# Conv, residual and a mixed 64x64 product per sample: each load queue takes one block of channels over the whole length, with fillers of TensorE moved and the last unit cut by half pairs

## The reference

```python
out0 = conv1d(x, weight, pad 4, 9 taps, 4 groups of 16 channels)    # weight: 64 x 16 x 9
x    = x + out0 + (cond @ c_weight.T)[:, :, None] + bias[None, :, None]
h    = gelu(cond @ W0 + b0); h = gelu(h @ W1 + b1)
att  = softmax(h @ W2 + b2)                                         # 8 experts, per sample
mix  = einsum('bk,koi->boi', att, W)                                # a 64x64 matrix per sample
x    = x + einsum('boi,bih->boh', mix, x) + (att @ bias_k)[:, :, None]
```

## Time and profile before

| | us |
|---|---|
| median of 3 executions | 248.54 (248.18 to 249.06) |
| the profiled execution, whole | 249.11 |
| the profiled execution, span | 247.3 |
| TensorE busy within the span | 237.3 (96%) |
| VectorE busy | 220.3 (89%) |
| ScalarE busy | 126.6 (51%) |
| GpSimd busy | 10.4 (4%) |

### The profile page before, as it was taken

How to read it: one execution, slowest core, us unless ns; L and a number is a source line. 1 busy time by engine, 2 the same in 40 slices (tenths; PEclk the granted TensorE clock), 3 DMA queues, 4 the chain that set the end, 5 groups by cost and what they waited for, 6 DMA issues and landing times.

```text
span 247.3 us, 5763 instructions
## 1 busy us (share of the span) xinstructions
PE 237.3 (96%) x2162; PEld 103.9 (42%) x2162; DVE 220.3 (89%) x113; ACT 126.6 (51%) x208; POOL 10.4 (4%) x36
## 2 busy tenths in 40 slices
PE   6799999999999999999999999999999999999991
PEld 4643334344344444444444444444444444444530
DVE  1075899999999999999999999999999999999582
ACT  2457007374535456383645445373745446263772
POOL 1325000000000000000000000000000000000000
PEclk9689999999999999999999999999999999999999
DMA  7998566999999999999999999999999997444448
GB/s 189 307 326 240 152 125 191 258 312 365 357 322 268 359 263 383 249 380 238 334 294 292 327 256 378 247 388 239 362 273 322 298 281 293 170 170 172 171 184 328
DMA packets 28555, 68.39 MB, mean 277 GB/s; under 512 B 3184, under 2 KB 3568, under 8 KB 28544
## 3 DMA queue, kind: packets, MB, share of 16 engines
q1 hardware_dynamic: 19104, 50.98, 62.3%
q10 hardware_dynamic: 9440, 17.26, 26.5%
HBM read 34.67 MB, written 33.55 MB: 276 GB/s over the span
## 4 chain that ended last, share of the span: by engine, by line
PE 91%; DVE 3%; ACTq 2%; ACT 1%; issue 1%; DVEq 0%
PE yps L528 64%; PE zps L551 21%; PE yps L608 3%; DVE ynat L433 2%; ACTq L285 2%; PE yps L565 1%; PE zps L577 1%; DVE ycol L424 1%; PE yps L509 0%; PE yps L623 0%; PE yps L588 0%; ACT mixt L317 0%; DVE xin L498 0%; PE zps L588 0%; ACT L324 0%
## 5 line engine op out<-in xcount | busy, mean ns | idle before, releaser
L528 PE MATMUL yps<-xph,wraw 64*64 64x512 f32 x1512 | 169.0, 589 | 0.0
L303 ACT ACTIVATE zout<-zps,gamu 128x512 f32<-128x512 f32 x120 | 72.7, 688 | 95.3 <-PE zps L551 75.6
L528 PEld LDWEIGHTS yps<-xph,wraw 64*64 64x64 f32 x1512 | 67.5, 132 | 94.0 <-issue 94.0
L424 DVE STREAM_TRANSPOSE ycol<-yps 128x1024 f32<-128x1024 f32 x63 | 75.2, 1224 | 7.0 <-PE yps L528 5.4
L402 DVE STREAM_TRANSPOSE xph<-xin 128x4160 f32<-128x4160 f32 (+2 forms) x17 | 71.7, 4220 | 5.1 <-DMA xin<-in_x 5.1
L433 DVE STREAM_TRANSPOSE ynat<-ycol 128x4096 f32<-128x4096 f32 x15 | 66.7, 4446 | 1.1
L551 PE MATMUL zps<-ynat,mixv 64*64 64x512 f32 x480 | 57.8, 589 | 0.3 <-DVE ynat L433 0.3
L312 ACT ACTIVATE mixv<-mixt 64x256 f32 (+1 forms) x64 | 42.4, 663 | 1.4 <-ACT mixt L317 0.2
L551 PEld LDWEIGHTS zps<-ynat,mixv 64*64 64x64 f32 x480 | 21.6, 133 | 29.9 <-issue 29.6
L608 PE MATMUL yps<-zout 128*128 128x256 f32 x26 | 10.4, 566 | 1.3 <-POOL zout L243 1.3
L241 POOL COPY gamu<-gam 128x4 f32 (+1 forms) x16 | 2.9, 188 | 199.9 <-ACT zout L303 191.8
(11 more groups left out here) (56 smaller groups left out, 34.8 us busy)
## 6 DMA issues: line engine op xcount, KB each, us to landing
out<-zout SPq DMA_DIRECT2D x60, 512.0 KB, 6.2
xin<-in_x SPq DMA_DIRECT2D x64, 258.0 KB, 7.2
xin<-in_x ACTq DMA_DIRECT2D x64, 258.0 KB, 7.4
out<-xin SPq DMA_DIRECT2D x2, 512.0 KB, 2.7
out<-xin SPq DMA_DIRECT2D x4, 256.0 KB, 3.0
mlps<-in_mlp SPq DMA_DIRECT2D x1, 233.5 KB, 2.8
wraw<-in_conv_w ACTq DMA_DIRECT2D x1, 208.0 KB, 3.7
zout<-in_const_w SPq DMA_DIRECT2D x1, 160.0 KB, 9.3
```

The lines of the kernel that those rows point to most:

```text
L303: nc.scalar.activation(zout[:, o].rearrange("p (i c j q) -> p c i j q", i=2, c=2, q=PH)[:, c], zps[:, at:at + BANK].rearrange("p (q i j) - ...
L424: nc.vector.transpose(ycol[:, :, :, :, :, g].rearrange("p i s j q c -> p (i s j) q c"), yps[:, 2 * BANK * (g % 2):2 * BANK * (g % 2) + 2 * ...
L528: last = nc.tensor.matmul(yps[C * c:C * c + C, at:at + BANK].rearrange("p (s f) -> p s f", s=S // 2), wsum[rows, b, g], xph[slot][rows, g, ...
```

## The change

- **Loads.** SP brings block k = 0 of the channels and ACT block k = 1, each for both halves of the length. Order within a queue: samples t = 0 with half 0 and half 1, then t = 1 with half 0 and half 1. The DMAs are the same 128 pieces.
- **ScalarE's start.** The dummy Gelu stands right behind `conv_w`'s issue, ahead of `mix_w` and x of unit 0. ACT's part of unit 1 is issued as two DMAs behind `h1` and two behind `beta`.
- **Fillers.** One more behind the first two products of the chain, one more behind the product for `h2`; of the three behind `output_constants`, two move ahead of it and one stays.
- **The last unit.** All four pairs are mixed, emptied and stored by half pairs, in the order of `LAST`. ScalarE empties the first six, VectorE the last two; SP issues eight stores of 256 KB in place of two of 512 KB and four of 256 KB.

```diff
+LAST = (0, 0), (2, 0), (0, 1), (2, 1), (1, 0), (3, 0), (1, 1), (3, 1)
 def z_half(o, i):
-    return (yps, zps)[i][:, BANK * (o - 1):BANK * (o - 1) + 2 * BANK].rearrange(
-        "p (c h f) -> p h c f", c=2, h=2)[:, 0]
+    bank, at = {(0, 0): (zps, 0), (2, 0): (yps, 2), (0, 1): (zps, 2), (2, 1): (zps, 0),
+                (1, 0): (yps, 0), (3, 0): (yps, 2), (1, 1): (zps, 2), (3, 1): (zps, 0)}[o, i]
+    return bank[:, BANK * at:BANK * at + 2 * BANK].rearrange("p (c h f) -> p h c f", c=2, h=2)[:, 0]
 # SyncE: load
-                for k in range(KQ):
-                    for t in range(2):
-                        sp.dma_start(*x_piece(slot, u, 0, k, t)).then_inc(x_in[slot], 16)
+                for t in range(2):
+                    for i in range(2):
+                        sp.dma_start(*x_piece(slot, u, i, 0, t)).then_inc(x_in[slot], 16)
 # SyncE: stores of the last unit
+            for n, (o, i) in enumerate(LAST):
+                sp.wait_ge(z_act if n < 6 else z_dve, n % 6 + 1)
+                sp.dma_start(z_rows(NU - 1, o)[:, H * i:H * i + H], out_half(o, i)).then_inc(z_out[o], 16)
 # ScalarE
+            def load_sample(u, slot, t):
+                for i in range(2):
+                    act.dma_start(*x_piece(slot, u, i, 1, t)).then_inc(x_in[slot], 16)
             act.dma_start(wraw[0:C], conv_w).then_inc(w_in, 16)
+            act.wait_ge(zeroed, 1)
+            nc.scalar.activation(warm[:], warm[:], ACT.Gelu)
             act.dma_start(mixw, mix_w).then_inc(mix_in, 16)
             load(0, 0)
-            act.wait_ge(zeroed, 1)
-            nc.scalar.activation(warm[:], warm[:], ACT.Gelu)
-            load_block(1, 1, 0)
             act.wait_ge(mlp_in, 16)
             act.wait_ge(mm, 1)
             nc.scalar.activation(h1, sps[:, 0:NS], ACT.Gelu, bias=b0s).then_inc(act_mlp, 1)
-            load_block(1, 1, 1)
+            load_sample(1, 1, 0)
...
             nc.scalar.activation(beta[0:C], gps[0:C, 0:NS], ACT.Identity, bias=fsides[0:C]).then_inc(beta_made, 1)
+            load_sample(1, 1, 1)
 # ScalarE and VectorE: the last unit
+            for n, (o, i) in enumerate(LAST[:6]):
+                act.wait_ge(last_mixes, n + 1)
+                evacuate_half(o, i)
+            for n, (o, i) in enumerate(LAST[6:]):
+                dve.wait_ge(last_mixes, 7 + n)
 # TensorE: start
             nc.tensor.matmul(gps[0:C, 0:NS], cws, condt, start=True, stop=True).then_inc(beta_mm, 1)
+            keep_on(1)
             pe.wait_ge(act_mlp, 1)
             nc.tensor.matmul(sps[:, NS:2 * NS], w1s, h1, start=True, stop=True).then_inc(mm, 1)
+            keep_on(1)
...
             aggregates()
+            pe.wait_ge(agg_out, 1)
+            keep_on(2)
             output_constants()
-            keep_on(3)
+            keep_on(1)
 # TensorE: the last unit
             pe.wait_ge(mixv_made, 4 * NU)
+            pe.wait_ge(last_nat, 1)
+            pe.wait_ge(z_made, 8 * NU - 10)
+            mix_half(0, 0)
+            pe.wait_ge(last_cols, 2)
+            mix_half(2, 0)
             pe.wait_ge(last_nat, 2)
-            pe.wait_ge(z_made, 8 * NU - 10)
-            mix_first(0)
             pe.wait_ge(z_made, 8 * NU - 8)
-            mix_first(2)
+            mix_half(0, 1)
+            pe.wait_ge(z_act, 1)
+            mix_half(2, 1)
             pe.wait_ge(last_nat, 3)
             pe.wait_ge(last_cols, 4)
             mix_half(1, 0)
+            pe.wait_ge(z_act, 2)
             mix_half(3, 0)
             pe.wait_ge(last_nat, 4)
-            pe.wait_ge(z_act, 2)
+            pe.wait_ge(z_act, 3)
             mix_half(1, 1)
             pe.wait_ge(z_act, 4)
             mix_half(3, 1)
```

More of the change, by code:

```diff
@@ L159, in y_last @@
                 "p (i h f) -> p h i f", i=2, h=2)[:, 0]
-        def z_first(o):
-            return zps[:, BANK * o:BANK * o + 2 * BANK].rearrange("p (c f) -> p c f", c=2)
         def z_half(o, i):
-            return (yps, zps)[i][:, BANK * (o - 1):BANK * (o - 1) + 2 * BANK].rearrange(
-                "p (c h f) -> p h c f", c=2, h=2)[:, 0]
+            bank, at = {(0, 0): (zps, 0), (2, 0): (yps, 2), (0, 1): (zps, 2), (2, 1): (zps, 0),
+                        (1, 0): (yps, 0), (3, 0): (yps, 2), (1, 1): (zps, 2), (3, 1): (zps, 0)}[o, i]
+            return bank[:, BANK * at:BANK * at + 2 * BANK].rearrange("p (c h f) -> p h c f", c=2, h=2)[:, 0]
         def out_last(o):
@@ L223, in _ @@
                     store(u, o)
[L224 to L228, removed]
+            for n, (o, i) in enumerate(LAST):
+                sp.wait_ge(z_act if n < 6 else z_dve, n % 6 + 1)
                 sp.dma_start(z_rows(NU - 1, o)[:, H * i:H * i + H], out_half(o, i)).then_inc(z_out[o], 16)
             for o in range(PR):
-                sp.wait_ge(z_out[o], 16 * NU + 16 * (o % 2))
+                sp.wait_ge(z_out[o], 16 * NU + 16)
         @block.gpsimd
@@ L282, in _ @@
         def _(act):
-            def load_block(u, slot, k):
-                for t in range(2):
-                    act.dma_start(*x_piece(slot, u, 1, k, t)).then_inc(x_in[slot], 16)
+            def load_sample(u, slot, t):
+                for i in range(2):
+                    act.dma_start(*x_piece(slot, u, i, 1, t)).then_inc(x_in[slot], 16)
             def load(u, slot):
@@ L291, in load @@
                     act.wait_ge(turned, 1 if isinstance(u, int) and u == 2 else u)
-                for k in range(KQ):
-                    load_block(u, slot, k)
+                for t in range(2):
+                    load_sample(u, slot, t)
             def evacuate(u, slot, o):
@@ L376, in _ @@
             act.wait_ge(turned, NU)
[L378 to L382, removed]
             def evacuate_half(o, i):
@@ L495, in _ @@
             dve.wait_ge(gam_cut, NU)
-            for n, o in enumerate((1, 3)):
-                dve.wait_ge(last_mixes, 5 + n)
+            for n, (o, i) in enumerate(LAST[6:]):
+                dve.wait_ge(last_mixes, 7 + n)
                 nc.vector.tensor_scalar(
-                    out_half(o, 1).rearrange("p (c j q) -> p c j q", c=2, q=PH),
-                    z_half(o, 1).rearrange("p c (q j) -> p c j q", q=PH),
+                    out_half(o, i).rearrange("p (c j q) -> p c j q", c=2, q=PH),
+                    z_half(o, i).rearrange("p c (q j) -> p c j q", q=PH),
                     gamu[1][:, o:o + 1], None, ALU.add).then_inc(z_dve, 1)
@@ L570, in conv_last @@
                 last.then_inc(last_conv, 1)
[L572 to L581, removed]
             def mix_half(o, i):
@@ L589, in mix_half @@
                             z_half(o, i)[C * s:C * s + C, c].rearrange("p (n j) -> p n j", j=NJ),
-                            mixv[1][rows, 2 * o + s], ynat[1][rows, o // 2, :, i, 2 + s],
+                            mixv[1][rows, 2 * o + s], ynat[1][rows, o // 2, :, i, 2 * (o % 2) + s],
                             start=True, stop=True)
```

## The result

| | us |
|---|---|
| before, median of 6 executions | 248.66 (248.18 to 249.06) |
| changed, median of 6 executions | 253.37 (252.56 to 255.17) |
| ratio | 1.0187 (95% interval 1.0168 to 1.0205) |
| profiled execution of the changed kernel: whole, span | 253.01, 251.2 |

What follows compares the result with a forecast made beforehand. TensorE fills 91% of the chain, so only start and end can move the time. Start +2.1, middle 0 and end -0.8 give +1.3 us, so 249.8 us from a median of 248.54; forecast range 248.9 to 252.2, 8-in-10 range 245.8 to 252.6.

Steps and rivals of the forecast that it cites:

- The sign, the place and the mechanism of the loss: Start: both queues collide on half the partitions, unit 1 lands late and TensorE waits; slower, +2.1 us there.
- Rival 2: Start: no collision, slow stretches came from a single queue or engines drift apart; start gains 1.6, total 246.1; chance 0.31.
- Rival 3: Start: partial collision, f about 0.35; +0.9 from the start, -0.8 from the end, total 248.6; chance 0.15.
- f: Start's loads: share of bytes moved at 204 GB/s because both queues are on the same half; taken as 0.5.
- the sum: Start: first convolution at 19.2 plus 2.3 us wait for unit 1, less 19.43, gives +2.1 us; +5.9 with f = 1.
- const_w and the clock: Start: const_w keeps the fillers' chain from ending before 16.5; a clock that stays up takes 1.6 us off the fillers.
- rival 4: The middle too: slow loads delay stores, or first convolutions run at 1.2 GHz; 3 us and more, 253 and up; chance 0.12.
- The third group's wait: Start: unit 1 lands at 23.2, 2.3 us late for unit 0's third group, and TensorE stands still for that.
- The due time of unit 1: Start: unit 1 may land 1.7 us after the first convolution starts, at 20.9, since VectorE needs 2.38 + 1.25 us.
- The start with f = 0: Start without any collision: -1.6 us, as unit 1 then costs 0.2 of the 1.8 that TensorE's side offers.
- The middle at 0: Middle: TensorE doesn't wait for loads and late stores have about 4 us of room; 0, bounds 0 and +1.5 us.
- The end at -0.8: End: earlier first mix and half-pair stores from 238.7 finish at 246.1 against 246.8; -0.8 us, bounds -0.3 and -1.4.

Runs made afterwards that it cites:

- e5: Changed kernel with each load piece on every eighth of all 128 partitions, from 4i + 2k + t on: 253.53 us, ratio 1.0200.
- e9: As e5, but a piece's first partition is 4k + 2i + t, so the two queues never meet on one set: 247.51 us, ratio 0.9967.
- e12: Changed kernel with const_w issued ahead of x of unit 0 in SP's queue: 252.74 us, ratio 1.0176.
- e7: Kernel before, with ACT's queue reading the first half of the length too, into its own partitions: 249.03 us, ratio 1.0008.
- e11: Kernel before with the change's last unit alone (half pairs, eight stores of 256 KB): 247.48 us, ratio 0.9956.
- e2: Changed kernel with the loads divided as before; ScalarE's start, fillers and last unit are the change's: 247.45 us, ratio 0.9941.
- e3: Kernel before with the change's division of the loads for units 0 and 1 alone: 254.83 us, ratio 1.0239.
- e10: Kernel before, with each load piece on every eighth partition from 4k + 2i + t on: 255.94 us, ratio 1.0305.
- e1: Kernel before with the change's division of the loads alone, for all units: 254.55 us, ratio 1.0248.
- e6: Changed kernel with a piece's 16 rows read 4 KB apart in device memory in place of 64 KB: 252.71 us, ratio 1.0174.
- e8: Changed kernel with ACT's queue reading the other half of the length than the one whose partitions it writes: 253.44 us, ratio 1.0197.

## Why the prediction was right or wrong

- **The sign, the place and the mechanism of the loss were right.** The two queues collide on a set of partitions (of which the half is one case, e5 and e9), units 0 and 1 land late, VectorE's wait for unit 1 holds back unit 0's third group. Rival 2 (no collision) had 0.31 and was wrong; its reading "a single queue is slow" is refuted by 220 GB/s with two queues. Rival 3 fell with it.
- **The term that was mis-sized is f**, the share of bytes that goes at the low rate: 0.5 assumed. With 204 as the low rate, 215 in place of 260 from 5 to 9 us makes 0.76, 213 in place of 329 from 9 to 14 us 0.89, and 220 in place of 350 from 14 to 18 us 0.83. The landings say the same: units 0 and 1 were 6.4 us late in all, where the sum has 7.6 us for f = 1, which makes 0.85. That is the sum's own size for f; the rates and the landings are two readings of one trace. The step that failed was "and I take f = 0.5, as engines drift apart too", with the distance "of up to half a piece": no run shows the engines apart, and the rates show the two queues on one set for most of the bytes. The measured start is +4.9 in place of +2.1, and the formula with 0.85 gives +4.7. The range for f that the forecast took ended at 0.8, below what was measured. In e12's profile, with SP's pieces further behind, the 249 GB/s make f 0.57; by this one execution more distance helps, but the changed kernel doesn't have it.
- **What the profile of before stood for.** The forecast adds its terms to a profile whose first mix was at 35.85; e7 and e11, with the same instructions at the start (e7 only reads other columns), had it at 34.79 and 35.09. Taken from these, the start costs 5.7 to 6.0 us, and less the end's 1.0 that is near the 4.7 between the medians. Carrying the span's +3.9 over to the median of 248.54 gives 252.4, 0.9 below the 253.37 measured. That the executions of before start earlier in most cases is argued from three profiles, not counted.
- **const_w and the clock**: the prediction had `const_w` as a bound at 16.5 and didn't carry on that it stands behind unit 0 in the same queue, and is late when unit 0 is. It ended the first convolution's wait at 21.74, not unit 0 (turned at 20.78), and the granted clock was 0.50 from 18 to 21. Both are covered by unit 1, by the 1.11 us that TensorE still waited for it. The clock was named under rival 4.
- **The third group's wait**: 2.3 us forecast, 1.1 measured, since the first two groups started at 21.74 in place of 19.2, behind `const_w`, and took 6.60 at the lower clock in place of 5.39, while unit 1 landed 2.6 us later than forecast. The due time of unit 1, 3.6 us ahead of the third group's start, was right: 25.80 and 29.45.
- **The start with f = 0** was put at -1.6 and is -0.7 in e2. Unit 1 was taken to land as before, at 19.4, and landed at 20.1 in e2 and in e11; it is the bound there too. `h1` came 0.5 us earlier (5.62 for 6.11) in place of 1.1, and `h2` in the changed kernel not at all (7.55 for 7.41).
- **Rival 4** had 253 and up, and the measured 253.37 lies there, but not by its mechanism: the middle cost nothing (e3, e10), and the low clock in the first convolutions, which did come, was covered by unit 1.
- **The middle at 0**: right (e3). The stores of pairs 2 and 3 issued at 106.8 and 107.9 landed 11.1 us later in place of 7.4, by the row below, and used most of the 4 us of room. Unit 3's load wasn't late.

```profile
DMA to landing us min/median/max: 11.0/11.1/11.3
```

- **A slip in the range.** By the prediction's own sum f = 0.42 gives 249.2, not 248.9; the lower end would need f = 0.38. It changes nothing, since the measured time lies above the range.
- **The end at -0.8**: right, 1.0 in the profile, 1.1 in e11. The first mix of the last unit no longer waits, and eight stores follow ScalarE's half pairs. Timeline of the changed kernel's end, answering to rows 10:

```profile
243.36 4.96 SPq L225 DMA_DIRECT2D out<-xin  x8
```

  The last was issued at 247.8 and landed 2.9 us later, against 3.0 before.

## What to carry to other kernels

When two DMA queues load at one time, look at which partitions their transfers stand on at the same moment, not only at how the bytes are shared out; keep the two queues on sets that don't meet, as the kernel before did by giving each queue one half. A load's place in the order is cheap to change while it has room, but in a start that waits for the loads the rate counts in full: unit 1 came 9.5 us after unit 0 in place of 6.3. Fillers and an earlier table load bought nothing here, where the next thing waited for was a load. Before a change of the start is forecast from one profile, look at the clock and the first convolution in another execution. The kernels with the loads of before and the change's last unit, with or without the rest of the change (e2, e11), both take 247.5 us; no kernel here that loads the data to their right places was faster.

## What the runs showed of the hardware

- Pieces on every second partition of 32 went at 203 GB/s with one queue alone (before, 31 to 34 us) and at 209 to 222 with two queues mostly on the same half (14 to 18 us: e1, e3, the changed kernel, e6, e8). Pieces on every eighth partition of 128 went at 210 and 215 with two queues mostly on the same set (e10, e5). Two queues on sets that don't meet went at 327 to 350 (before, e2, e7, e9, e11). The 16 DMA engines were fully taken in all of these. The Trainium skill's rule on ports ("SBUF — State Buffer", section "Door 1: The DMA port swizzle") agrees: e5, e9 and e10 follow its map. The same page of the Trainium skill, section "Can I just issue two DMAs to hit both halves?", has two DMAs at one time, on partitions 0 and 64, at only 6% over one; the trace disagrees: here two queues on the two halves moved 70% more than one, 350 GB/s against 203.
- Where the places are read in the device's memory made no difference that these runs can tell: rows 4 or 64 KB apart (e6, 222 GB/s for 220), the same or other halves of a row (e7, 349 for 350; e8, 218 for 220).
- In the middle, from 60 to 220 us, the DMA engines' busy share was 1.03 in e1, e10 and the changed kernel and 0.97 in before, and TensorE was busy for all of the 160 us in each: stores that come later let ACT's loads run beside them. That this is what evens it out was argued, not tried by itself.
